# Moving three stationary operands of TensorE to other places modulo 512 bytes in on-chip memory

## The reference

```
x = X + attention(layernorm(X))
    Q = xpos(n @ W_Q); K = xpos(n @ W_K, downscale); V = n @ W_V          (256 -> 256)
    p = softmax(Q K^T) * 0.9**|i - j|;  attention = p V                     (2048 x 2048 a batch)
x = x + ffn(layernorm(x))
    gate = q4(n) @ q4(w_gate)^T; up = q4(n) @ q4(w_up)^T                    (256 -> 704)
    ffn  = q4(silu(gate) * up) @ q4(w_down)^T                              (704 -> 256)
q4: per block of 16, scale = max|x| / 6, round x / scale to 0, .5, 1, 1.5, 2, 3, 4, 6
```

## Time and profile before

| | |
|---|---|
| median of 3 runs | 2571.62 us (2568.94 to 2575.65) |
| the profiled execution | 2572.08 us, of which span 2570.3 us |
| granted TensorE clock, mean | 0.997 |
| PE busy | 99% of the span |
| PEld busy | 89% |
| DVE, ACT, POOL busy | 84%, 59%, 71% |
| chain that ended last | PE 81% |

### The profile page before, as it was taken

One profiled execution on the slowest core, in us unless ns is written; L12 is line 12 of the kernel. 1 busy time (PEld: TensorE's weight loads), 2 busy tenths in 40 slices (PEclk: granted clock), 3 DMA queues, 4 the chain that ended last, 5 costly groups with the idle time before them and its releaser, 6 DMA issues.

```text
span 2570.3 us, 51983 instructions
## 1 busy us (share of the span) xinstructions
PE 2535.4 (99%) x16188; PEld 2293.8 (89%) x16188; DVE 2148.3 (84%) x4784; ACT 1505.4 (59%) x2966; POOL 1819.8 (71%) x1919
## 2 busy tenths in 40 slices
PE   9999989999999999999999999999999999999998
PEld 8888879999999999989999899989999999989997
DVE  8999868888888888788888888888888888888886
ACT  5666555566656655656555665566566656565654
POOL 6999947667766767667766766667766776667665
PEclk9999999999999999999999999999999999999999
DMA  8777510113111311131111311131113111221110
GB/s 286 278 282 283 192 55 23 44 34 109 40 46 30 110 42 46 32 106 44 34 42 53 98 32 46 36 108 38 46 32 106 44 42 34 78 74 40 38 38 22
DMA packets 163474, 203.29 MB, mean 79 GB/s; under 512 B 15184, under 2 KB 116752, under 8 KB 163216
## 3 DMA queue, kind: packets, MB, share of 16 engines
q1 hardware_dynamic: 163216, 200.01, 24.0%
HBM read 103.42 MB, written 77.59 MB: 70 GB/s over the span
## 4 chain that ended last, share of the span: by engine, by line
PE 81%; DMA 1%; issue 1%; SPq 1%; DVE 1%; POOL 1%; ACT 1%; DVEq 0%; ACTq 0%; POOLq 0%
PE score L483 26%; PE acc L615 19%; PE ring L483 18%; PE acc L483 8%; PE ring L583 6%; PE ring L635 3%; DMA keys<-k_dram 1%; PE ring L574 1%; PE acc L657 1%; SPq L414 1%; ACT probs L783 0%; POOL h_buf L962 0%; POOL h_buf L956 0%; POOL hq_buf L969 0%; DVE h_buf L1250 0%
## 5 line engine op out<-in xcount | busy, mean ns | idle before, releaser
L483 PE MATMUL score<-keys,q_st 128*128 128x512 f32 x3072 | 761.3, 396 | 7.1 <-ACT probs L783 3.4
L483 PEld LDWEIGHTS score<-keys,q_st 128*128 128x128 f32 x3072 | 559.6, 189 | 117.3 <-issue 3.8
L615 PE MATMUL acc<-vals,pT 128*128 128x256 f32 x3984 | 557.1, 287 | 0.8 <-DVE pT L1154 0.8
L941 POOL TENSOR_TENSOR probs<-probs,decay 128x512 f32<-128x512 f32 (+3 forms) x416 | 446.9, 1087 | 144.4 <-ACT probs L783 144.4
L483 PE MATMUL ring<-w_gu,xqT 128*128 128x512 f32 (+1 forms) x2304 | 509.1, 374 | 0.0
L615 PEld LDWEIGHTS acc<-vals,pT 128*128 128x128 f32 x3984 | 499.2, 189 | 6.1 <-DVE pT L1154 2.0
L483 PEld LDWEIGHTS ring<-w_gu,xqT 128*128 128x128 f32 x2304 | 418.6, 188 | 63.2
L753 ACT ACTIVATE pT<-ring 128x512 fp32r<-128x512 f32 (+3 forms) x432 | 226.9, 535 | 380.2 <-PE ring L583 372.7
L1167 DVE TENSOR_REDUCE smax<-score 128x1 f32<-128x1024 f32 x256 | 312.4, 1220 | 105.7 <-PE score L483 104.8
L1154 DVE TENSOR_TENSOR pT<-ring,pT 128x512 fp32r<-128x512 f32 (+3 forms) x432 | 251.0, 606 | 69.0 <-ACT pT L753 67.9
L947 POOL TENSOR_TENSOR xv<-xv,xe 128x256 f32<-128x256 f32 x128 | 94.4, 738 | 274.0 <-DVE xv L1023 274.0
(11 more groups left out here) (132 smaller groups left out, 4619.9 us busy)
## 6 DMA issues: line engine op xcount, KB each, us to landing
k_dram<-keys SPq DMA_DIRECT2D x56, 512.0 KB, 4.7
keys<-k_dram SPq DMA_DIRECT2D x56, 512.0 KB, 7.5
edge<-vals SPq DMA_DIRECT2D x288, 64.0 KB, 2.1
q_raw<-q_dram SPq DMA_DIRECT2D x129, 128.0 KB, 2.6
x_in<-X SPq DMA_DIRECT2D x32, 512.0 KB, 4.5
q_dram<-q_stage SPq DMA_DIRECT2D x32, 512.0 KB, 5.6
x_res<-X SPq DMA_DIRECT2D x128, 128.0 KB, 2.1
out<-x_res SPq DMA_DIRECT2D x128, 128.0 KB, 1.7
```

The costliest lines, as they stand in the source:

```text
L483: mm = pe.matmul(dst, stat(a, k), mov(m, k), start=i == 0, stop=ends and i == n - 1)
L615: mm = pe.matmul(pv_out, pT[g % 2][:, a, j * P:(j + 1) * P], edge[place][:] if kb in edges else vals[m][:, kb, :], start=i == 0, stop=i == ...
L941: op = pool.tensor_tensor(probs[:, k0:k1], probs[:, k0:k1], decay[:, off + k0:off + k1], ALU.mult)
```

## The change

Only fillers are added or resized. No instruction, wait or DMA is added or taken away, and every tensor keeps its shape.

```
             x_in = [sb1(f"x_in{i}", [P, CT, D]) for i in range(2)]
+            gap("gap_qk", 10 * UNIT, sb1, 0)
             w_in = [sb1(f"w_in{i}", [P, KT, 2 * D], F32R) for i in range(2)]
-            gap("gap_w", LINE - 2 * UNIT, sb1, 0)
+            gap("gap_w", LINE - 2 * UNIT, sb1, 10 * UNIT)
             wv_in = [sb1(f"wv_in{i}", [P, KT, D], F32R) for i in range(2)]
-            gap("gap_x", 0, sb1, LINE - 2 * UNIT)
+            gap("gap_xT", 0, sb1, LINE - 2 * UNIT)
...
         q_raw = [sb(f"q_raw{i}", [P, KT, P]) for i in range(2)]
+        gap("gap_q", LINE - 2 * UNIT, sb, 0)
         q_st = [sb(f"q_st{i}", [P, 2, KT, P], F32R) for i in range(2)]
+        gap("gap_x", 0, sb, LINE - 2 * UNIT)
         x_res = sb("x_res", [P, XR, D])
...
+        gap("gap_xq", LINE - 4 * UNIT, sb, 0)
         xqT = [sb(f"xqT{i}", [P, KT, P], F32R) for i in range(2)]
-        gap("gap_T", 2 * UNIT, sb, 0)
+        gap("gap_T", 2 * UNIT, sb, LINE - 4 * UNIT)
         hT = [sb(f"hT{i}", [P, HK, P], F32R) for i in range(2)]
```

## The result

The changed kernel takes 2584.28 us, the median of 5 runs (2582.69 to 2584.57), against 2571.95 us, also of 5 runs (2568.94 to 2575.65), for the kernel before. The ratio is 1.0044, 95% interval 1.0032 to 1.0055: slower by 0.44%, 12.3 us. The profiled execution took 2582.69 us with a span of 2580.8 us, 10.5 us more span than before, so the trace carries most of the difference. The forecast was 2559 us. The time lies in the stated range (2555 to 2588) and on the other side of no change.

The account below looks back on a forecast made before the run. The prediction took PE's own list of matmuls to bound the kernel. From the profiled 2572.08 us it took off 3.8 (queries) and 9.0 (quantised rows), with 0 for projection weights: 2559.3, stated as 2559 us, range 2555 to 2588.

Parts of the forecast that it names:

- What bounds the kernel: Whole kernel: PE's own list, busy 99%; time is the sum of distances between matmuls, floor 226.7 ns at 512 columns.
- The sign of the excess at distance 0: Score and gate burst heads, both operands at 0: first matmuls 395 to 397 ns against 389, taken as removable excess.
- the first case: Faster as forecast: excess from moving read meeting the next load's read, depending on their distance modulo 512; 2559 us, chance 0.43.
- the second rival: Excess stays about as large: new distances change which matmul pays, or one pair gains what another loses; 2571 us, chance 0.34.
- the sign for states handed on: Values product: a mean group length that moves would mean the burst before sets the state of the next.
- Quantised rows, 128 in front of the gate weights: Gate and up product, 2304 matmuls: head and six 384-column matmuls come to the floor, -0.07 x 128 = -9.0 us.
- My upper bound for the part: Gate and up product: 5 ns standing on 2304 matmuls, 11.5 us, less 9.0, so +2.5 us.
- I take -3.8: Scores, queries 64 bytes in front of keys, 3072 matmuls: all heads settle at once, -0.03 x 128 = -3.8 us.
- I take 0: Stage 1 projection, weights 192 in front of the rows, 768 matmuls: burst already at the floor, 0; bounds -4.6 to +3.8 us.
- The slower rival: All three moved products: new distances never settle, 5 ns on 6144 matmuls, +17.9 us, 2590 us; chance 0.23.
- Its decision point: Slower case: it decides from 12.8 us / 6144 matmuls = 2.1 ns of mean excess a matmul on.

Follow-up runs that it names:

- both_moved: Kernel before, with queries and keys both moved to 448 and quantised rows and gate and up weights both to 384, distance still 0; 2572.08 us, ratio 0.9998.
- xq_only: Kernel before, with only the quantised rows moved, 128 bytes in front of the gate weights; 2581.16 us, ratio 1.0035.
- plus64: Kernel before, with queries, quantised rows and projection weights all at 64 modulo 512, moving operands at 0; 2586.16 us, ratio 1.0054.
- other_side: Kernel before, with queries at distance -32, rows +96, projection weights +224, and the 256-column pairs at 128; 2605.76 us, one time.
- narrow_96: Kernel before, wide pairs at 0, with values at distance 96, down product at 160, projection of values at 32; 2594.09 us, one time.
- narrow_192: Kernel before, wide pairs at 0, with down, values and projection of values moved from distance 64 to 192; 2581.34 us, ratio 1.0036.

## Why the prediction was wrong

*What bounds the kernel* held. PE stayed at 99%, the loss is in its busy time, and the floor of 226.7 and 113.3 ns is not undercut as a standing value in any run. Nothing in the writes of the moved operands shows in the time (`both_moved`).

*The sign of the excess at distance 0* is where it broke. I read the head of 395 to 397 ns as what a distance of 0 costs, and its removal as a gain of 0.03 us a score burst. The head did go (226 instead of 233), as the first case said. But it was the price of getting into step after a burst of another kind, and at 0 a burst gets into step. At the new distances it never does: 392 ns standing for the scores (394 as the median of the whole trace), 394 for the gate product's wide matmuls. The row that said so was in front of me. The stage 1 burst, with both operands at 0, has no head, and I used it for the floor and gave its reading to the second rival. In the best case, behind a fast down burst, a score burst gains 7 ns (2746 against 2753) and not 30; behind a slow one it loses 47 (2800). That a group with a median above 389 would show the forecast wrong stood in the prediction, and so did the sign for states handed on, a group length of the values that moves: it went from 287 to 286 ns.

*The failed step, in the prediction's words: "Quantised rows, 128 in front of the gate weights ... I take -9.0."* Alone this part measured +0.35% (0.21 to 0.49), 9 us. Of that 5.7 us is the 512-column matmuls, whose mean length rose from 392 to 395. The six of 384 columns did get cheaper, but by 1 ns each (339 to 338), 0.7 us in all, where the forecast had them come down from 1063 ns a tile to 6 x 170, 43 ns less. And 2.9 us by its group row, some 3.3 by its bursts, is the down product, which no term of the sum had. My upper bound for the part, +2.5 us, was too low twice over: it set the head's and the third piece's 9 us off against the standing excess as if both would go at once, and it left out the burst behind.

*Queries: "I take -3.8."* Measured 0 (-2.8 to +2.1 us by the interval). The scores lost on their second burst (20 ns each, 2.5 us), won 7 ns on the first, and the values behind them won 1.8 us by their group row. *Projection weights: "I take 0"* came out right in the sum, and only there, by luck: the projection's bursts grew by 3.9 us in all and the values projection's shrank by 2.9. No part of my argument had this. In time these two parts came out as the second rival has it, that a burst pays elsewhere or one product loses what another gains.

*The slower rival* is what happened in kind: the new distances never settle. Its price was 5 ns on 6144 matmuls, +17.9 us. Measured in group means it is +2 ns on the scores, +4 on the 512-column and -1 on the 384-column gate matmuls, +6 on the projection: 2 x 3072 + 4 x 1536 - 768 + 6 x 768 = 16.1 us. The down product adds 2 x 1920 = 3.8; the values (287 to 286 ns) and the projection of values (281 to 277 and 278) take off 4.0 and 2.7. That is 13 us, where the medians of the runs are 12.3 apart; the closeness is in part luck, since the means are whole nanoseconds and half of one is 2 us on the 3984 values matmuls alone. Summed over the trace from start to start, with the few distances above 1 us counted as 1 us, the scores have +4.8 us, the gate product +6.6 and -0.8, the down product +5.3, the projection +1.9 (it waited less), the values -2.2 and the projection of values -3.9: 11.7 us against 10.5 of span. Its decision point, 2.1 ns of mean excess a matmul, was worked out from a gain that didn't exist.

*The rule of the Trainium skill* ("SBUF — State Buffer", section "Who interferes with whom": PE has two independent read ports and "PE and ACT never wait on anyone") would have given 2572 us. Runs `xq_only` and `plus64`, with no instruction more or less, took 1.0035 and 1.0054 times as long as the kernel before, so the distance between PE's own two operands does matter here, and the measurement decides.

What stays open: what in the chip makes a period of 256 bytes, why the length of the stream (256, 384 or 512 columns) decides which distance settles, and what a state is. The runs show that it is handed on from burst to burst on PE and that the operands' distance and the stream's width rule how it moves; I have no run that looks inside. The changed kernel has 53 steps with a slow down burst and the kernel with the rows alone has 29; what puts a step into one kind or the other lies before the gate burst (in the changed kernel its first distance is 225 or 226 ns in the 69 fast steps and mostly 224, 234 or 235 in the 53 slow ones) and isn't traced further. That the changed kernel's 12.3 us against the rows' 9 come from these extra slow steps and the score bursts behind them is argued from one trace of each; the two intervals of the times overlap.

## What to carry to other kernels

On a kernel whose time is TensorE's own list, the distance between the stationary and the moving operand, modulo 256 bytes, is worth up to 1.3% here (2572 us against the single 2606 us of `other_side`), and it costs nothing but filler. Read it off the start-to-start distances within one burst, and judge a placement by the whole length of all bursts of a kind, not by the first matmuls of one: the gate burst's head that ends (3810 ns) is cheaper than its excess that stays (3846), while a score burst of 12 with the small standing excess takes 2746 ns behind a fast down burst and 2800 behind a slow one, against 2753 with the head. Then look at the next burst too, because a product that wasn't touched may win or lose as much as the one that was.

## What the runs showed of the hardware that I had not expected

- The distance between starts of matmuls with 32-bit operands in back-to-back bursts settles at 226.7 ns for 512 columns and 113.3 ns for 256, at a granted clock of 1.00 (2.4 GHz): the same 0.443 ns a column. Above it lies an excess, in medians of up to 14 ns a matmul (241 against 227 in the changed kernel's gate burst) and in one run of 20 (133 against 113, down product of `narrow_96`), that depends on the distance of the operands and on what ran before.
- Equal bursts with equal operands have more than one stable pace: 113.3 or some 118 ns for 256 columns at a distance of 64 bytes (lengths 276 and 281). In the changed kernel both occur in one execution, and each of the 53 score bursts behind a slow down burst is slow, while 68 of the 69 behind a fast one aren't.
- The entry into the steady pace at distance 0, after a first matmul or two, goes through the same sequence in most bursts that follow one of 256 columns: 236, 224, 231, 236, 228, 232, 231, 227 ns, or a tail of it. In `narrow_192` the gate burst begins 235, 233, 236, 224, 231, 236, 228, 232, 231, 227; in the kernel before 233, 236, 228, 232, 231, 227. Behind transposes it is only near this: 314, 231, 231, 235, 227, 232, 231, 227.
